# Attention kernel on one core: five of eight value tiles as three fp32r products instead of one fp32 product

## The chip, the cores and the metric

The kernel runs on one core of one Trainium2 chip. The metric is the device time in microseconds of one execution. A core has TensorE (PE: matmuls, and PEld: its weight loads), VectorE (DVE), ScalarE (ACT), GpSimd (POOL) and SyncE (SP, which here only starts DMAs). Each engine works through its own list of instructions in order; semaphores order the engines against each other.

## The reference

One block of a network: gated cross-attention and then a gated feed-forward part with quantised weights. Batch 2, 512 queries of 512 channels, a context of 1024 keys of 128 channels, 16 heads. Cut to what matters (`kv_rope` is both key and value):

```python
q_r = einsum('bshq,hqr->bhsr', q_big, W_qr)        # queries, 64 numbers per head
k_r = einsum('bld,hdr->bhlr', kv_rope, W_kr)       # keys, 64 numbers per head
scores = einsum('bhsr,bhlr->bhsl', q_r, k_r)
attn = softmax(scores)
ctx_c = einsum('bhsl,bld->bhsd', attn, kv_rope)    # the value product
out = einsum('bhsd,hkd->bshk', ctx_c, w_kc_kv).reshape(b, s, H * K) @ Wo.T
x = x + tanh(g_xattn) * out
x = x + tanh(g_ffn) * ffn(layernorm(x))            # rmsnorm, ternary weights, silu gate
```

## The kernel before, in words

**Tiling.** Heads go in eight pairs (p = 0 to 7). A pair has four units (w = 0 to 3): a unit is one batch and half of the queries. A unit's probabilities are four tiles t of 128x1024 in `E`. The main loop walks slots: slot (p, w) has eight steps c = 0 to 7. In it TensorE does the value product of unit w from the turned probabilities `G` (`pv_matmul`, L1383, one key tile of 128 keys for each step, an fp32 product), and everything else works ahead: the second half of unit w + 2 (tiles 2 and 3; "u2") and the first half of unit w + 3 (tiles 0 and 1; "u3").

**One tile's way.** TensorE makes its scores (`score_matmuls`, L1360; two banks `ps_s`, so the scores of the next two tiles wait for the exponentials of the last two). DVE takes the row maximum (`max_tile`, L1755), ACT the exponential with its sum (`exp_tile`, L1580), DVE the reciprocal (`inv_tile`, L1760), GpSimd scales the tile (`pool_scale`, L1160), DVE turns its 32x32 blocks (`turn_blocks`, L1765). When the four tiles of a unit are turned and the value product of the unit that used the buffer is over, SP starts 16 DMAs from `E` to `G` (`exchange`, L1096); the value product of that unit runs in the next slot. The first exponential of u3 waits for that exchange, since it writes `E` again.

**DVE's order in a slot** (`dve_pair`): reciprocal of u3's tile 1 from the slot before, turn tile 0, `ctx_lo`, turn tile 1, low parts of side tasks, maxima of u2's tiles 2 and 3, their reciprocals, turn tile 2, read of an `out` product, turn tile 3, maxima of u3's tiles 0 and 1, another `out` read, reciprocal of tile 0. In pairs 4 to 6 two roundings of feed-forward weights (`round_half`, L1781) stand in front of the turn of tile 2.

**ACT's order** (`act_pair`): `ctx_high` at step 0, high parts of side tasks (`side_high`, L1536), exponentials of u2's tiles 2 and 3 at steps 2 and 3, of u3's tiles 0 and 1 at steps 6 and 7, and two halves of the feed-forward weights: absolute sums in pairs 0 to 3 ("sum") at steps 1 and 4, tanh in pairs 4 to 6 ("quant"), both at step 0.

**GpSimd's order** (`pool_pair`): the scalings of u2's tiles 1, 2, 3 and of u3's tile 0, nothing else but in a few slots.

**Side tasks** on TensorE between the steps, for the next pair: `m` and `a` (query matrix), `q`, `k` (keys: three fp32r products of `wk_hi`, `wk_lo` with `kvT_hi`, `kvT_lo`, L1322 to L1324), `b` (output matrix) and `out` (L1265 to L1267: six fp32r products). An exact fp32 value is kept there as a high part (its fp32r rounding) and a low part (the rest), and a product is high x high, low x high and high x low.

Of the kernel before, what the change touches and what calls it, by code (L numbers as in the profile page):

```python
# [181 lines left out]
def build(nc, A):  # L182
    with ExitStack() as ctx:
# [983 lines left out]
        def xn_low(pool, b):  # L1167

            pool.wait_ge(side_done, side_index(0, "first", ("q", b)) + 1)
            for i in (2 * b, 2 * b + 1):  # L1170
                hi, lo, full = xn_half(i)
                pool.wait_ge(xn_high, i + 1)
                nc.gpsimd.tensor_tensor(lo, full, hi.bitcast(F32), ALU.subtract).then_inc(xn_split, 1)

        def join_xn(pool, b):
# [2 lines left out]
            for h in range(2):
                hi, lo, _ = xn_half(2 * b + h)
                whole = xn_rows[:, b, h * DT // 2:(h + 1) * DT // 2, :].rearrange("p c s -> p (c s)")  # L1180
                nc.gpsimd.tensor_tensor(whole, hi.bitcast(F32), lo.bitcast(F32), ALU.add).then_inc(xn_joined, 1)

        def pool_pair(pool, p, last=False):
            for w in range(4):
                second, first = not (last and w >= 2), not (last and w >= 1)
                for at, t in enumerate((1, 2, 3, 0)):
                    if second if t else first:
                        pool_scale(pool, *unit_ahead(p, w, 2 if t else 3), t)
                    if at == 0:
                        if is0(p) and w in XN_LOW_SLOTS:  # L1190
                            xn_low(pool, XN_LOW_SLOTS.index(w))
                        for b in range(BATCH):
                            if isinstance(p, int) and (p, w) == XN_JOIN_SLOTS[b]:
                                join_xn(pool, b)
                    if last and (w, at) == (1, 2):
                        ln2_root(pool, 0)
                if last and w == 1:
                    atanh_end(pool)
# [798 lines left out]
```

## Time and profile before

| | us |
|---|---|
| median of 3 runs (lowest, highest) | 673.21 (672.68, 674.67) |
| the profiled execution | 677.15 |
| its span, first to last instruction | 675.4 |
| busy PE / DVE / ACT / POOL | 653.5 / 543.9 / 356.8 / 259.7 |
| granted TensorE clock, mean | 0.995 |

The page of the profile gives busy time by engine, the span in 40 slices, the chain of work that ended last, and the costliest groups. The timeline gives each instruction's start, duration and, in brackets, how long its engine stood idle before it and what released it. Durations of matmuls include the time in the array, so the distance between starts is the cost of one. A waiting instruction holds up all that its engine has behind it.

### The profile page before, as it was taken

How to read it: one execution, taken by the hardware profiler on the slowest of the kernel's cores; microseconds unless marked ns; L12 is line 12 of the kernel's file. 1: busy time of each engine (PE TensorE's matmuls, PEld its weight loads, DVE VectorE, ACT ScalarE, POOL GpSimd, SP SyncE). 2: the span in 40 equal slices, each digit the busy share in tenths (PEclk: the TensorE clock that was granted, in tenths of full speed). 3: DMA queues.
4: the chain of work that ended last, by engine and by line, in shares of the span. 5: the costliest groups of instructions: out<-in, count | busy, mean ns of one | idle time of the engine just before them, and what ended most of it. 6: DMA issues, size and time to landing. Idle time of an engine off the chain costs nothing.

```text
span 675.4 us, 9297 instructions
## 1 busy us (share of the span) xinstructions
PE 653.5 (97%) x2870; PEld 377.5 (56%) x2870; DVE 543.9 (81%) x882; ACT 356.8 (53%) x571; POOL 259.7 (38%) x232
## 2 busy tenths in 40 slices
PE   9798999999999999999999999999999898999997
PEld 8564555665665555565655555555555454445553
DVE  5787877788868885888698979997999886998873
ACT  3564664455445544554545454545454533498875
POOL 4822265133223222322235443332333352686651
PEclk9999999999999999999999999999999998999999
DMA  8108885788498849884988688869688763000001
GB/s 299 63 1 218 234 226 117 226 237 228 108 241 243 220 105 243 231 215 109 239 245 207 184 225 237 212 168 238 163 214 230 172 149 101 1 0 32 17 33 48
DMA packets 45206, 112.77 MB, mean 167 GB/s; under 512 B 11888, under 2 KB 15088, under 8 KB 45040
## 3 DMA queue, kind: packets, MB, share of 16 engines
q1 hardware_dynamic: 43712, 110.01, 61.5%
q10 hardware_dynamic: 1392, 2.29, 1.0%
q8 instruction: 19, 0.31, 0.2%
q14 instruction: 19, 0.16, 0.1%
q0 software_dynamic: 64, 0.00, 0.0%
HBM read 45.16 MB, written 2.10 MB: 70 GB/s over the span
## 4 chain that ended last, share of the span: by engine, by line
PE 48%; DVE 30%; ACT 7%; SPq 6%; POOL 3%; issue 3%; DMA 2%; PEld 1%; POOLq 0%; DVEq 0%; ACTq 0%; PEldq 0%
DVE E L1765 9%; PE ps_b L1392 9%; PE ps_s L1371 7%; DVE small L1755 7%; PE ps_ctx L1392 7%; ACT E L1580 6%; SPq L1096 5%; PE ps_s L586 5%; DVE wq L1781 2%; PE ps_b L1265 2%; POOL E L1160 2%; DVE x_sb L1745 2%; PE ps_b L1267 2%; PE ps_b L637 2%; PE ps_b L1266 2%
## 5 line engine op out<-in xcount | busy, mean ns | idle before, releaser
L1160 POOL TENSOR_SCALAR E<-E,small 128x1024 f32<-128x1024 f32 x128 | 151.1, 1190 | 346.7 <-DVE small L1760 346.6
L1580 ACT ACTIVATE E<-ps_s,small 128x1024 f32<-128x1024 f32 x128 | 142.3, 1113 | 209.0 <-DVE small L1755 177.5
L1765 DVE STREAM_TRANSPOSE E<-E 128x1024 f32<-128x1024 f32 x124 | 152.8, 1233 | 27.9 <-POOL E L1160 27.8
L1755 DVE TENSOR_REDUCE small<-ps_s 128x1 f32<-128x1024 f32 x128 | 149.1, 1203 | 4.5 <-PE ps_s L1371 4.4
L1392 PE MATMUL ps_ctx<-G,kv 128*128 128x512 f32 x256 | 123.2, 599 | 0.0
L1392 PE MATMUL ps_b<-G,kv 128*128 128x512 f32 x256 | 119.9, 598 | 2.1 <-DMA G<-E 2.1
L1392 PEld LDWEIGHTS ps_b<-G,kv 128*128 128x128 f32 x256 | 48.0, 190 | 51.8 <-issue 46.0
L1392 PEld LDWEIGHTS ps_ctx<-G,kv 128*128 128x128 f32 x256 | 46.4, 189 | 43.0 <-issue 40.3
L1265 PE MATMUL ps_b<-b_hi,ctx_hi 128*128 128x512 f32 x128 | 66.4, 519 | 0.6 <-DVE ctx_lo L1717 0.6
L1371 PE MATMUL ps_s<-k_hi,q_hi 64*128 64x512 f32 x256 | 57.3, 443 | 4.6 <-ACT E L1580 3.6
L586 PE MATMUL ps_s<-wq,q12T 128*128 128x512 fp8e4 x256 | 61.1, 385 | 0.1
L1371 PE MATMUL ps_s<-k_hi,q_lo 64*128 64x512 f32 x256 | 51.1, 393 | 0.0
L1371 PE MATMUL ps_s<-k_lo,q_hi 64*128 64x512 f32 x256 | 50.8, 392 | 0.0
L1267 PE MATMUL ps_b<-b_lo,ctx_hi 128*128 128x512 f32 x128 | 50.4, 393 | 0.0
L1266 PE MATMUL ps_b<-b_hi,ctx_lo 128*128 128x512 f32 x128 | 50.2, 392 | 0.0
L524 POOL TENSOR_TENSOR hg<-h_f,E 128x512 f32<-128x512 f32 x32 | 40.4, 1270 | 25.1 <-DVE h_f L932 25.1
L1745 DVE SCALAR_TENSOR_TENSOR x_sb<-ps_b,small,x_sb 128x512 f32<-128x512 f32 x62 | 44.6, 720 | 4.7 <-PE ps_b L1267 4.7
L1760 DVE RECIPROCAL small<-small 128x1 f32<-128x1 f32 x128 | 19.3, 156 | 31.0 <-ACT E L1580 24.7
L1371 PEld LDWEIGHTS ps_s<-k_hi,q_hi 64*128 64x128 f32 x256 | 24.1, 183 | 32.6 <-issue 19.1
L586 PEld LDWEIGHTS ps_s<-wq,q12T 128*128 128x128 bf16 x256 | 24.4, 99 | 28.3 <-issue 4.1
L1265 PEld LDWEIGHTS ps_b<-b_hi,ctx_hi 128*128 128x128 f32 x128 | 24.0, 188 | 23.1 <-issue 15.3
L1266 PEld LDWEIGHTS ps_b<-b_hi,ctx_lo 128*128 128x128 f32 x128 | 24.1, 189 | 10.5 <-issue 7.7
(199 smaller groups left out, 960.9 us busy)
## 6 DMA issues: line engine op xcount, KB each, us to landing
G<-E SPq DMA_DIRECT2D x496, 128.0 KB, 2.4
w_stage<-in_wffn SPq DMA_DIRECT2D x48, 512.0 KB, 4.4
wo_s<-in_woT SPq DMA_DIRECT2D x8, 512.0 KB, 5.3
wq_s<-in_wq SPq DMA_DIRECT2D x7, 512.0 KB, 6.3
wkcq_s<-in_wkcqT SPq DMA_DIRECT2D x7, 384.0 KB, 4.5
out<-x_sb SPq DMA_DIRECT2D x8, 256.0 KB, 2.0
x_sb<-in_x SPq DMA_DIRECT2D x3, 512.0 KB, 5.9
wqr_s<-in_wqr SPq DMA_DIRECT2D x7, 192.0 KB, 5.4
```

What stands on the lines that cost most here:

```text
L524: nc.gpsimd.tensor_tensor(hg[:, k, cols], h_f[:, k, cols], g3[:, cols], ALU.mult).then_inc(hg_done, 1)
L586: last = nc.tensor.matmul(ps_s4[:, 2 * i + c % 2, :], q12T[:, k, i, d, :], wq8[:, DT * i + d, cols], start=(d == 0), stop=(d == DT - 1))
L1160: nc.gpsimd.tensor_scalar(e, e, rowinv[:, k:k + 1], 1.0, ALU.mult, ALU.mult).then_inc(scaled, 1)
L1265: nc.tensor.matmul(into, ctx_hi[:, cols], b_hi[:, h, :], start=(h == 0), stop=False)
L1266: nc.tensor.matmul(into, ctx_lo[:, cols], b_hi[:, h, :], start=False, stop=False)
L1267: last = nc.tensor.matmul(into, ctx_hi[:, cols], b_lo[:, h, :], start=False, stop=(h == 1))
L1371: last = nc.tensor.matmul(ps_s[:, h, cols], q[head, b, rows], k[head, b, cols], start=(i == 0), stop=(i == 2))
L1392: last = nc.tensor.matmul(CTX_PS[w % 2].rearrange("p (t i q) -> p t i q", t=ST, i=4), kv[:, w // 2, c, :], turned, start=(c == 0), stop=(c ...
L1580: nc.scalar.activation(out, scores, ACT.Exp, bias=negmax[:, k:k + 1], accum_out=rowsum[:, k:k + 1]).then_inc(exp_done, 1)
L1745: last = nc.vector.scalar_tensor_tensor(x, bank_in, g_tanh[:, 0:1], x, ALU.mult, ALU.add)
L1755: nc.vector.tensor_reduce(negmax[:, k:k + 1], ps_s[:, t % 2, :], AX_X, ALU.max, negate=True).then_inc(max_done, 1)
L1765: nc.vector.transpose(e_tile(w % 2, t), e_tile(w % 2, t)).then_inc(blocks_turned, 1)
```

## The change

It does these things:

- In pairs 0 to 6 the value product of key tiles 0 to 4 is three fp32r products (`kv_hi` x high, `kv_lo` x high, `kv_hi` x low) instead of one fp32 product; tiles 5, 6, 7 stay fp32. The steps take the tiles in the order 5, 0, 6, 1, 2, 3, 7, 4. Pair 7 stays all fp32.
- ACT makes the high part of each of the five tiles (`split_high`, a copy of 128x512), into one of three places; those of tiles 0, 1, 2 at step 0, of tile 3 at step 2 behind the exponential of u2's tile 2, of tile 4 at step 4.
- GpSimd makes the low parts (`split_low`, a subtraction of 128x512). Its order in a slot becomes: scale u2's tile 1, low 0, low 1, low 2, low 3, scale u2's tiles 2 and 3, low 4, scale u3's tile 0. The splitting and joining of `xn` is spread out ahead of the last one.
- GpSimd cuts `kv` in high and low parts before the loop (`cut_kv`) and joins them before pair 7 (`join_kv`).
- The `k` task becomes one fp32 product of the whole `wkr_s` and `kvT`. The high and low parts of the key weights (`wk_high`, `wk_low`) and the low part of `kvT` go away; SP's load of the next key weights waits for the last `k` task, in the third slot.

The diff, cut:

```diff
+SPLIT = 5
+HIGH_PLACE = (0, 2, 1, 0, 1)
+STEP_TILE = (5, 0, 6, 1, 2, 3, 7, 4)
+HIGH_STEPS = (0, 0, 0, 2, 4)
...
+        def split_low(pool, p, w, i):
+            tile = g_tile(w % 2, i)
+            pool.wait_ge(split_hi, SPLIT * 4 * p + (SPLIT * w + i + 1))
+            pool.sem_inc(pool_passed, 1)
+            nc.gpsimd.tensor_tensor(g_tile(w % 2, i, G_lo), tile, high_part(i).bitcast(F32).rearrange("p (t i q) -> p t i q", t=ST, i=4),
+                                    ALU.subtract).then_inc(split_lo, 1)
...
         def pool_pair(pool, p, last=False):
             for w in range(4):
                 second, first = not (last and w >= 2), not (last and w >= 1)
...
+                u2, u3 = unit_ahead(p, w, 2), unit_ahead(p, w, 3)
+                if is0(p) and w == 0:
+                    split_low(pool, p, w, 0)
+                if second:
+                    pool_scale(pool, *u2, 1)
...
+                if not (last or is0(p) and w == 0):
+                    split_low(pool, p, w, 0)
+                if not last:
+                    split_low(pool, p, w, 1)
...
+                if not last:
+                    split_low(pool, p, w, 2)
+                if not last:
+                    split_low(pool, p, w, 3)
+                if second:
+                    pool_scale(pool, *u2, 2)
+                    pool_scale(pool, *u2, 3)
...
+                if not last:
+                    split_low(pool, p, w, 4)
+                for i in range(2 * BATCH):
+                    if is0(p) and w == XN_LOW_SLOTS[i]:
+                        xn_low(pool, i)
+                    if isinstance(p, int) and (p, w) == XN_JOIN_SLOTS[i]:
+                        join_xn(pool, i)
+                if isinstance(p, int) and (p, w) == (PAIRS - 2, 3):
+                    join_kv(pool, 0)
+                if first:
+                    pool_scale(pool, *u3, 0)
...
+            if tile < SPLIT and not (isinstance(p, int) and p == PAIRS - 1):
+                high = high_part(tile).rearrange("p (t i q) -> p t i q", t=ST, i=4)
+                pe.wait_ge(split_lo, SPLIT * 4 * p + (SPLIT * w + tile + 1))
+                nc.tensor.matmul(into, kv_hi[:, b, tile, :], high, start=(c == 0), stop=False)
+                nc.tensor.matmul(into, kv_lo[:, b, tile, :], high, start=False, stop=False)
+                last = nc.tensor.matmul(into, kv_hi[:, b, tile, :], g_tile(w % 2, tile, G_lo), start=False, stop=(c == LT - 1))
+                if tile < SPLIT - 1:
+                    last.then_inc(split_done, 1)
+            else:
+                last = nc.tensor.matmul(into, kv[:, b, tile, :], turned, start=(c == 0), stop=(c == LT - 1))
...
+        def split_high(act, p, w, i):
+            used = 4 * (SPLIT - 1) * p + (SPLIT - 1) * w
+            if i == 0:
+                if is0(p) and w == 0:
+                    act.wait_ge(kv_cut, 6)
+                else:
+                    act.wait_ge(split_done, used)
+                act.wait_ge(exchanged[w % 2], 2 * EXCHANGE * p + EXCHANGE * (w // 2 + 1))
+            elif i == 2:
+                if not (is0(p) and w == 0):
+                    act.wait_ge(pv_done, 4 * p + w)
+            elif i == 3:
+                act.wait_ge(split_done, used + 1)
+            elif i == 4:
+                act.wait_ge(split_done, used + 3)
+            copy_act(high_part(i).rearrange("p (t i q) -> p t i q", t=ST, i=4), g_tile(w % 2, i)).then_inc(split_hi, 1)
...
                 for c in range(LT):
+                    if c == 0 and variant != "last":
+                        split_high(act, p, w, 0)
...
-                    if (w, c) == WK_AT and variant != "last":
-                        wk_high(act, 16 * p + 32)
+                    for i in range(1, SPLIT):
+                        if c == HIGH_STEPS[i] and variant != "last":
+                            split_high(act, p, w, i)
...
-                nc.tensor.matmul(into, wh, kvT_hi[:, b, cols], start=True, stop=False)
-                nc.tensor.matmul(into, wl, kvT_hi[:, b, cols], start=False, stop=False)
-                last = nc.tensor.matmul(into, wh, kvT_lo[:, b, cols], start=False, stop=True)
+                last = nc.tensor.matmul(into, wkr_s[:, :, :].rearrange("p a r -> p (a r)"), kvT[:, b, cols], start=True, stop=True)
...
-                    if (w, c) == WK_AT and variant != "last":
-                        wk_low(dve, p + 2)
```

## Rows read from the trace of the kernel before

**Rows 1.** The page's first part: busy time by engine over the whole span.

```profile
PE 653.5 (97%) x2870; PEld 377.5 (56%) x2870; DVE 543.9 (81%) x882; ACT 356.8 (53%) x571; POOL 259.7 (38%) x232
```

**Rows 2.** Windows, pair 2's four slots: length, busy PE, PEld, DVE, ACT, POOL; clock, DMA.

```profile
182.74:202.53 19.79, 19.79 (x93) 12.65 (x92) 13.83 (x22) 7.56 (x14) 4.46 (x5) 1.00 0.78 206
202.53:218.30 15.77, 15.77 (x66) 9.64 (x65) 13.39 (x19) 8.55 (x16) 4.45 (x5) 1.00 0.89 242
218.30:233.71 15.41, 15.41 (x61) 8.73 (x60) 12.89 (x17) 8.39 (x15) 4.46 (x5) 1.00 0.88 227
233.71:248.71 15.00, 15.00 (x61) 8.75 (x61) 12.39 (x16) 7.91 (x15) 4.47 (x5) 1.00 0.59 133
```

**Rows 3.** The same view, pair 6's four slots.

```profile
452.12:472.01 19.89, 19.48 (x84) 11.37 (x83) 15.24 (x22) 10.32 (x18) 4.73 (x5) 1.00 0.83 218
472.01:488.45 16.44, 16.44 (x65) 9.22 (x63) 15.23 (x20) 7.46 (x13) 5.12 (x5) 1.00 0.60 161
488.45:504.63 16.18, 16.18 (x62) 8.82 (x61) 14.57 (x19) 8.33 (x14) 5.22 (x5) 1.00 0.84 214
504.63:520.22 15.59, 15.59 (x62) 8.31 (x62) 13.97 (x19) 7.81 (x13) 5.22 (x5) 1.00 0.86 232
```

**Rows 4.** The same view, pairs 0, 1, 3, 4 and 5 whole.

```profile
49.46:117.03 67.57, 64.97 (x253) 35.41 (x252) 52.82 (x73) 38.41 (x68) 28.30 (x22) 1.00 0.77 199
117.03:182.74 65.71, 65.71 (x276) 39.51 (x275) 52.59 (x73) 32.13 (x58) 17.85 (x17) 1.00 0.77 204
248.71:316.55 67.84, 66.74 (x281) 40.12 (x280) 53.10 (x76) 32.36 (x59) 17.82 (x16) 1.00 0.77 197
316.55:384.76 68.21, 67.62 (x290) 41.00 (x290) 57.27 (x80) 31.89 (x52) 24.75 (x19) 1.00 0.80 212
384.76:452.12 67.36, 67.20 (x264) 37.34 (x263) 58.64 (x79) 33.78 (x55) 25.53 (x19) 1.00 0.81 215
```

**Rows 5.** Timeline of DVE, the last slot of pair 2.

```profile
237.35 2.35 DVE L1755 TENSOR_REDUCE small<-ps_s 128x1 f32<-128x1024 f32 x2
239.84 0.16 DVE L1760 RECIPROCAL small<-small 128x1 f32<-128x1 f32 x1
241.36 1.25 DVE L1765 STREAM_TRANSPOSE E<-E 128x1024 f32<-128x1024 f32 x1 [0.22 <-POOL E L1160]
248.71 1.25 DVE L1765 STREAM_TRANSPOSE E<-E 128x1024 f32<-128x1024 f32 x1 [0.60 <-POOL E L1160]
```

**Rows 6.** Timeline of ACT and of POOL, the same slot.

```profile
238.61 1.11 ACT L1580 ACTIVATE E<-ps_s,small 128x1024 f32<-128x1024 f32 x1 [1.21 <-DVE small L1755]
...
240.21 2.27 POOL L1160 TENSOR_SCALAR E<-E,small 128x1024 f32<-128x1024 f32 x2 [5.43 <-DVE small L1760]
```

**Rows 7.** Chain of waits: start, length, what; fp32 value products and one fp32r product.

```profile
206.94 3.43 PE ps_b L1392 x8
...
269.29 0.23 PE ps_b L1345
```

**Rows 8.** Groups of instructions: busy us, mean ns; idle before.

```profile
L524 POOL TENSOR_TENSOR hg<-h_f,E 128x512 f32<-128x512 f32 x32 | 40.4, 1270 | 25.1 <-DVE h_f L932 25.1
L1536 ACT ACTIVATE xnT<-xn_rows 128x1024 fp32r<-128x1024 f32 x2 | 2.1, 1052 | 0.0
```

**Rows 9.** Timeline of DVE and ACT, the first slot of pair 2.

```profile
190.25 0.69 DVE L1717 TENSOR_TENSOR a_lo<-ps_b,a_hi 128x512 fp32r<-128x512 f32 x1 [1.84 <-ACT a_hi L1536]
...
197.58 1.11 ACT L1580 ACTIVATE E<-ps_s,small 128x1024 f32<-128x1024 f32 x1 [5.81 <-DMA G<-E]
```

**Rows 10.** Timeline of ACT and DVE, third slot of pair 6: the second `k` task.

```profile
490.69 0.58 ACT L1536 ACTIVATE k_hi<-ps_b 128x512 fp32r<-128x512 f32 x1
...
491.94 0.65 DVE L1717 TENSOR_TENSOR k_lo<-ps_b,k_hi 128x512 fp32r<-128x512 f32 x1
```

**Rows 11.** Instructions of the rounding's line: shortest, median, longest ns; first and last start.

```profile
L1781 DVE TENSOR_SCALAR wq<-w_stage x24: 669/702/1499, 343.5 to 527.5; 128x1024 fp8e4<-128x1024 f32 x24
```

**Rows 12.** Timeline of SP: the 16 DMAs of one exchange.

```profile
217.55 10.04 SPq L1096 DMA_DIRECT2D G<-E  x16
```

More of the change, by code:

```diff
@@ L1124, in sp_pair @@
                     load_wq(sp, p + 2)
-                    sp.wait_ge(wk_ready, p + 2)
+                if w == 2 and not (variant == "last" or isinstance(p, int) and p == 6):
+                    sp.wait_ge(side_done, side_index(p, variant, ("k", 1, 1)) + 1)
                     load_kr(sp, p + 2)
@@ L1165, in xn_half, with xn_low @@
             return tuple(x.rearrange("p c s -> p (c s)") for x in (XNT[b][:, 0, part, :], XNT[b][:, 1, part, :], XNT_FULL[b][:, part, :]))
[L1167 to L1175, printed above, removed]
-            pool.wait_ge(side_done, side_index(XN_JOIN_PAIR, "mid", ("q", b)) + 1)
[L1178 to L1181, printed above, removed]
+        def xn_low(pool, i):
+            pool.wait_ge(side_done, side_index(0, "first", ("q", i // 2)) + 1)
+            hi, lo, full = xn_half(i)
+            pool.wait_ge(xn_high, i + 1)
+            nc.gpsimd.tensor_tensor(lo, full, hi.bitcast(F32), ALU.subtract).then_inc(xn_split, 1)
@@ L1185, in pool_pair @@
                 second, first = not (last and w >= 2), not (last and w >= 1)
[L1186 to L1198, printed above, removed]
+                u2, u3 = unit_ahead(p, w, 2), unit_ahead(p, w, 3)
[3 more added lines that the diff above has]
+                    pool_scale(pool, *u2, 1)
+                if last and w == 0:
+                    join_kv(pool, 1)
+                if not (last or is0(p) and w == 0):
+                    split_low(pool, p, w, 0)
+                if not last:
+                    split_low(pool, p, w, 1)
+                if last and w >= 2:
+                    ln2_root(pool, w - 2)
+                if last and w == 3:
+                    rms_root(pool, 1)
+                if not last:
[5 more added lines that the diff above has]
+                    pool_scale(pool, *u2, 3)
                 if last and w == 2:
@@ L1248, in _ @@
                 pool_scale(pool, 0, 0, t)
-            for t in range(ST):
-                pool_scale(pool, 0, 1, t)
+            cut_kv(pool, 0)
+            pool_scale(pool, 0, 1, 0)
+            pool_scale(pool, 0, 1, 1)
+            cut_kv(pool, 1)
+            pool_scale(pool, 0, 1, 2)
+            pool_scale(pool, 0, 1, 3)
             pool_scale(pool, 0, 2, 0)
@@ L1315, in side_matmuls @@
                 _, b, j = task
[L1316 removed]
+                pe.wait_ge(ld_kr, 16 if at is not None else 16 * p + 32)
                 if at is not None:
@@ L1390, in pv_matmul @@
                     pe.wait_ge(ctx_done, 4 * p + (w - 1))
-            turned = G[:, w % 2, :, :, key_tile(c)].rearrange("p i t q -> p t i q")
-            last = nc.tensor.matmul(CTX_PS[w % 2].rearrange("p (t i q) -> p t i q", t=ST, i=4), kv[:, w // 2, c, :], turned,
-                                    start=(c == 0), stop=(c == LT - 1))
+            b, tile = w // 2, STEP_TILE[c]
+            turned, into = g_tile(w % 2, tile), CTX_PS[w % 2].rearrange("p (t i q) -> p t i q", t=ST, i=4)
+            if isinstance(p, int) and p == PAIRS - 1 and w in (0, 2) and c == 0:
+                pe.wait_ge(kv_joined, b + 1)
+            if tile < SPLIT and not (isinstance(p, int) and p == PAIRS - 1):
[8 more added lines that the diff above has]
+                last = nc.tensor.matmul(into, kv[:, b, tile, :], turned, start=(c == 0), stop=(c == LT - 1))
             if c == LT - 1:
```

86 lines of the change are left out of this document (47 added, 39 removed).

## The prediction

> **What bounds the kernel now.** First the busy times: PE is busy 97% of the span, DVE 81%, GpSimd 38% [rows 1]. Read alone, they say that every matmul saved is time saved. So the next view is the windows, with their edges where DVE turns tile 0 of a slot [rows 2 to 4]. PE is full in pairs 1 and 2 (65.71 us of 65.71 in pair 1) [rows 2, 4]. But DVE, busy only 13.4, 12.9 and 12.4 us in slots of 15.77, 15.41 and 15.00 [rows 2], has to be read by what its gaps wait for, and there the timeline decides. In the last slot of pair 2 DVE takes the two maxima at 237.35, ACT's exponential of tile 2 starts at 238.61, the reciprocal follows at 239.84, GpSimd's scaling at 240.21, DVE's turn of that tile at 241.36, idle until GpSimd was through [rows 5, 6]. That is a loop through DVE, ACT, GpSimd and back, and DVE starts nothing behind that turn before it. The gaps in slots 1 to 3 are all of this kind (a reciprocal that waits for an exponential, a turn that waits for a scaling); none waits for a matmul. Only in slot 0 does DVE wait for outsiders: 1.84 us at the `a` task, and ACT's exponential waits there for the exchange until 197.58, while its maximum was there by 196.6 [rows 9]. So there are two clocks of nearly the same length: PE's work, 66.0 us a pair, and DVE's loop. For the loop of a "sum" pair without outside waits I take slots 1 to 3 as they are (46.2 us) and about 18.6 for slot 0: 64.8. In pairs 4 to 6 the roundings fill DVE's gaps and the loop is the longer clock (68.1 in pair 6, with PE busy 67.7) [rows 3]. Whoever shortens PE alone gains about 1 us a pair; whoever lengthens the loop pays in every slot.
>
> **PE's part.** An fp32 tile costs 3.43 / 4 = 0.858 us (eight records, two a tile), an fp32r product 0.23 us [rows 7]; three make 0.69. Saved: 0.166 us a tile, 20 tiles a pair, 3.3 us; the four `k` tasks go the other way, 0.66 us. Net 2.66 us a pair, 18.6 us over seven pairs. On the path this is worth only what the loop leaves.
>
> **The loop's part.** In a slot GpSimd now does low 0 to 3 between the scaling of tile 1 and that of tile 2. Low 0 to 2 have 5.4 us of idle time to lie in [rows 6]: three subtractions at 1.27 us [rows 8] are 3.8, so they cost nothing. Low 3 doesn't: its high part stands on ACT behind the exponential of tile 2. So the scaling of tile 2, till now 240.21 - 238.61 = 1.60 us behind the start of that exponential [rows 6], comes after: exponential 1.14, high copy 0.6 (the row for twice the size is 1.05; I take 0.6, bounds 0.5 and 0.7), a semaphore's 0.1, low part 1.27 [rows 8]. That is 3.1 us, 1.5 later. The turn of tile 2 moves by the same 1.5, and the read of `out`, the turn of tile 3, the next maxima and exponentials are queued behind it on DVE: all of it shifts. In slot 1 a low part of a `k` task already stands in front of the reciprocal, so only 1.15 is added. In slot 0 two of these low parts (`a`, `k`) hide most of it: I count turn 2 at 9.85 us after turn 0 and 9.2 us from there to the next turn 0, 19.05, about what it was with its waits (19.79) [rows 2]. **Sum pair:** 19.05 + 15.77 + 15.41 + 15.00 + 1.15 + 1.5 + 1.5 = 69.4 us. PE needs 63.3 of these, so it waits now. Pair 1: +3.7, pair 2: +3.4, pair 3 (67.84, it had a late exchange that the idle PE would now absorb): +1.6 [rows 2, 4].
>
> **Quant pairs.** The same, plus two things. ACT has both tanh at step 0 and then the high part of the `k` or `q` task; three high copies now stand in front (1.55 us), and the distance between that task's high part (ready at 491.3) and its low part on DVE (491.94) covers 0.65 [rows 10]: 0.9 us more in slots 2 and 3. And the rounding. It takes 0.67 us with GpSimd silent and up to 1.50 beside it [rows 11]; low 3 now runs where it starts. On the other side the rounding used to fill part of the wait. I take +1.2 for the delay and the roundings, so +2.05 in slot 2 and +2.15 in slot 3, +1.3 in slot 1, +0.3 in slot 0: 5.8 us a pair for pairs 5 and 6. Pair 4 has no tanh in slot 0 and lost time there to an exchange: +4.7. Bounds for each of the nine quant slots: 0.7 (the rounding fills the whole wait) to 2.8.
>
> **Pair 0.** Slots 1 to 3 pay 1.15 + 1.5 + 1.5, and about 0.5 more, because ACT also splits `xn` there. In slot 0 low 0 stands before the scaling of tile 1, and TensorE's scores stand behind the product of tile 0: some 2.7 us, of which the exchange that the next exponential waits for hides a half. Together +6.1; bounds 3 and 9.
>
> **What costs nothing, and its cover.** `cut_kv` on GpSimd, some 3 us twice, lies in idle gaps of about 4 us between scalings. The prologue loses a few low parts on DVE and gets dearer `k` products: 0, within 1.5 either way. `join_kv` (1.6 us) lies in GpSimd's idle time. The `xn` splits before u3's scaling (2.4 us each) fit behind low 4. The later load of the key weights has a slot and more. The exchange needs 10.04 us of SP's starts and some 2.4 to land [rows 12]; slots become longer, so it has more room, and TensorE, now ahead of DVE, frees `G` earlier. Low 4 is ready about 12 us after turn 0, and tile 4 is the last step: TensorE ends a slot some 3 us before DVE, which is enough. Pair 7 and the feed-forward part have no splits: 0.
>
> **The sum.** 6.1 + 3.7 + 3.4 + 1.6 + 4.7 + 5.8 + 5.8 = 31.1 us. The profiled execution, 675.4 of span and 677.15 in all, would become 706.5 and 708.3. It lies 3.9 above the median of the runs; on that, 673.2 + 31.1 = **704.3 us**.
>
> **Rivals.** (1) Faster: the delay of the scaling is not paid, because low 3 gets its high part early or the shift is taken up by idle time that I read as part of the loop. Then the loop stays and only its outside waits go: 1 us a pair in pairs 1 and 2, 3 in pair 3, 1.5 in pair 4, near 666.5; were PE the only clock, 673.2 - 18.6 = 654.6. For it speaks PE at 97%; against it that no gap of slots 1 to 3 names a matmul. It decides below 0.4 us of delay a slot: three slots then use up the 1.2 that slot 0 has. Chance 0.12. (2) The same mechanism at half the price: quant slots at their lower bound of 0.7 (9 slots by 1.1 less, 10 us) and some of pair 0 hidden: 682 to 694. Chance 0.13. (3) Roundings and GpSimd exclude each other. The longest rounding, 1.50 us against 0.67 [rows 11], waited about 0.83 of a scaling that lasts 1.12, which looks like waiting for its end. Then the second rounding of a slot waits for the rest of low 3, or the scaling waits for the rounding, 0.6 more in nine or ten slots: 710. Chance 0.10. The Trainium skill states this as a rule (SBUF — State Buffer, "Who interferes with whom"): a DVE instruction in a 2-port mode and GpSimd take turns whole, the later one fully blocked. By that rule the row is no accident, and the price is this rival's. (4) TensorE falls behind because low 3 or low 4 is late, and the exchange with it: 716 to 728. Chance 0.04. (5) No change: 0.03. That the three products save PE nothing would change none of this, since PE's 66.0 would still be under 69.4.
>
> **How the numbers follow.** Forecast 0.58, at 696 to 712 by the bounds of the copy (0.1 us in 27 slots, 3 us), of the quant slots and of pair 0. The range takes in rival 3 and most of rival 2: 684 to 718, which leaves out 0.12 + 0.04 + 0.03 and a little. Slower by over 0.3% (what a measurement of this kernel can tell from no change): 0.58 + 0.13 + 0.10 + 0.04 = 0.85. Same 0.03, faster 0.12.
>
> **What the new profile would show.** Right: DVE's turn of tile 2 waits for POOL L1160, about 9.3 to 9.9 us after turn 0 where it was 7.65 in the last slot of pair 2; GpSimd's scaling starts right at the end of a low part, 3.1 us behind the start of the exponential; slots 1 to 3 of a sum pair are 16.5 to 17 us long; PE has waits on low parts or exponentials and is below 93% busy; the pair is 69 to 70 in "sum" and 72 to 74 in "quant". Wrong: if the pairs are 63 to 65 us long and PE still full, rival 1; if DVE waits for an exchange or a matmul in slots 1 to 3, rival 4; a low part of 128x512 well under 1.27 us would shrink all terms.

## The result

The changed kernel took **712.5 us** (median of 4 runs, 707.0 to 713.7), beside 673.1 (672.7 to 674.7) for the kernel before: a ratio of 1.0565, 95% interval 1.0508 to 1.0622, so 5 to 6% slower. Its profiled execution took 713.66 us with a span of 711.8.

The profile after, in the order of the views shown of before. The page's first part, busy time by engine (against [rows 1]):

```profile
PE 648.7 (91%) x2978; PEld 399.5 (56%) x2978; DVE 538.4 (76%) x870; ACT 424.5 (60%) x703; POOL 441.6 (62%) x380
```

Windows with their edges at DVE's turn of tile 0 (length, busy PE, PEld, DVE, ACT, POOL, granted clock, DMA share, GB/s): the four slots of pair 2, then of pair 6 (against [rows 2, 3]), then the first slots of pairs 0, 1 and 4:

```profile
197.79:216.80 19.01, 17.31 (x80) 11.40 (x79) 13.64 (x21) 10.65 (x21) 10.68 (x10) 1.00 0.80 217
216.80:233.79 16.99, 16.99 (x74) 10.71 (x74) 13.39 (x19) 10.09 (x19) 10.73 (x10) 1.00 0.87 236
233.79:250.77 16.98, 15.05 (x69) 10.12 (x67) 12.89 (x18) 10.82 (x21) 10.67 (x10) 1.00 0.83 213
250.77:267.15 16.38, 15.17 (x77) 10.23 (x77) 12.29 (x16) 10.19 (x20) 10.70 (x10) 1.00 0.44 100
...
484.43:503.72 19.29, 17.55 (x78) 11.00 (x75) 14.52 (x22) 12.67 (x23) 11.49 (x10) 1.00 0.81 217
503.72:521.46 17.74, 17.74 (x71) 10.29 (x71) 14.82 (x20) 9.97 (x17) 11.25 (x10) 1.00 0.67 173
521.46:539.73 18.27, 15.44 (x65) 9.28 (x61) 14.43 (x19) 10.77 (x19) 11.16 (x10) 1.00 0.72 181
539.73:557.53 17.80, 14.35 (x67) 8.81 (x67) 13.83 (x19) 10.30 (x18) 12.69 (x11) 1.00 0.82 214
...
48.69:73.04 24.35, 19.66 (x77) 11.43 (x76) 13.86 (x21) 13.47 (x26) 11.89 (x11) 0.86 0.73 186
...
124.30:147.44 23.14, 21.46 (x98) 14.82 (x98) 13.95 (x20) 9.95 (x19) 10.73 (x10) 0.93 0.73 197
...
336.89:357.50 20.61, 20.61 (x98) 14.47 (x97) 13.82 (x23) 10.36 (x20) 10.81 (x10) 0.95 0.77 202
```

DVE and TensorE are both less busy and the time is longer: neither is full, both wait. Slots 1 to 3 of pair 2 are 1.2, 1.6 and 1.4 us longer, those of pair 6 1.3, 2.1 and 2.2, and their first slots are 0.8 and 0.6 shorter. The first slots of pairs 0, 1 and 4 are long, and there the granted clock is below 1.00.

What a slot waits for stands in the timeline of its tile 2, here the third slot of pair 2 (ACT, then GpSimd, then DVE; in brackets the idle time and what ended it):

```profile
239.09 1.11 ACT L1674 ACTIVATE E<-ps_s,small 128x1024 f32<-128x1024 f32 x1 [2.05 <-DVE small L1847]
240.20 0.62 ACT L1615 ACTIVATE g_hi<-G 128x512 fp32r<-128x512 f32 x1
```

```profile
241.00 1.26 POOL L1226 TENSOR_TENSOR G_lo<-G,g_hi 128x512 fp32r<-128x512 f32 x1 [2.43 <-ACT g_hi L1615]
242.23 2.24 POOL L1182 TENSOR_SCALAR E<-E,small 128x1024 f32<-128x1024 f32 x2
```

```profile
243.40 1.25 DVE L1857 STREAM_TRANSPOSE E<-E 128x1024 f32<-128x1024 f32 x1 [1.29 <-POOL E L1182]
```

Exponential at 239.09, high copy, low part at 241.00, scaling at 242.23: 3.14 us behind the start of the exponential, where it was 1.60 [rows 6]. GpSimd sits idle for 2.43 us in front of the low part; the wait is for the copy on ACT, which stands behind the exponential. The groups over the whole span (busy us, mean ns; idle before):

```profile
L1226 POOL TENSOR_TENSOR G_lo<-G,g_hi 128x512 fp32r<-128x512 f32 x140 | 178.0, 1289 | 68.5 <-ACT g_hi L1615 66.1
L1857 DVE STREAM_TRANSPOSE E<-E 128x1024 f32<-128x1024 f32 x124 | 153.2, 1236 | 50.8 <-POOL E L1182 50.6
L1615 ACT ACTIVATE g_hi<-G 128x512 fp32r<-128x512 f32 x140 | 84.7, 629 | 0.6
L1438 PE MATMUL ps_s<-k_hi,q_hi 64*128 64x512 f32 x256 | 57.8, 446 | 21.7 <-ACT E L1674 20.6
```

DVE's turns wait 50.6 us for scalings, and TensorE's scores 20.6 us for exponentials, where it was 27.8 and 3.6 in the kernel before: TensorE waits for the loop, not the loop for TensorE.

### The profile page after: what moved, and what is told of

Same layout as the page of the kernel before. It is cut to its first block, busy times and chain, and to the rows that moved or that the text cites. A ratio compares the mean times of both kernels' runs of the same rounds, so it can differ in the third digit from the quotient of the medians.

```text
span 711.8 us, 10097 instructions
## 1 busy us (share of the span) xinstructions
PE 648.7 (91%) x2978; PEld 399.5 (56%) x2978; DVE 538.4 (76%) x870; ACT 424.5 (60%) x703; POOL 441.6 (62%) x380
## 4 chain that ended last, share of the span: by engine, by line
DVE 34%; PE 19%; ACT 16%; issue 13%; POOL 11%; SPq 4%; DMA 1%; DVEq 0%; POOLq 0%; ACTq 0%; PEld 0%
DVE small L1847 11%; DVE E L1857 10%; ACT E L1674 8%; POOL E L1182 7%; PE ps_s L607 5%; SPq L1117 4%; DVE x_sb L1841 3%; ACT g_hi L1615 2%; POOL G_lo L1226 2%; PE ps_b L658 2%; PE ps_s L1438 2%; ACT w_stage L1698 2%; PE ps_b L1408 2%; DVE ctx_lo L1813 1%; DVE k_lo L1813 1%
## 5 line engine op out<-in xcount | busy, mean ns | idle before, releaser
L1182 POOL TENSOR_SCALAR E<-E,small 128x1024 f32<-128x1024 f32 x128 | 149.1, 1177 | 133.9 <-DVE small L1852 133.9
L1226 POOL TENSOR_TENSOR G_lo<-G,g_hi 128x512 fp32r<-128x512 f32 x140 | 178.0, 1289 | 68.5 <-ACT g_hi L1615 66.1
L1857 DVE STREAM_TRANSPOSE E<-E 128x1024 f32<-128x1024 f32 x124 | 153.2, 1236 | 50.8 <-POOL E L1182 50.6
L1615 ACT ACTIVATE g_hi<-G 128x512 fp32r<-128x512 f32 x140 | 84.7, 629 | 0.6
L1438 PE MATMUL ps_s<-k_hi,q_hi 64*128 64x512 f32 x256 | 57.8, 446 | 21.7 <-ACT E L1674 20.6
L1472 PE MATMUL ps_ctx<-G,kv 128*128 128x512 f32 x116 | 60.4, 615 | 3.4 <-POOL xnT L1194 3.1
L1472 PE MATMUL ps_b<-G,kv 128*128 128x512 f32 x116 | 58.7, 594 | 2.0 <-DMA G<-E 2.0
L1336 PE MATMUL ps_b<-b_hi,ctx_hi 128*128 128x512 f32 x128 | 56.7, 443 | 1.1 <-DVE ctx_lo L1813 0.5
L1466 PE MATMUL ps_ctx<-g_hi,kv_hi 128*128 128x512 f32 x70 | 41.8, 598 | 15.8 <-POOL G_lo L1226 15.8
L1338 PE MATMUL ps_b<-b_lo,ctx_hi 128*128 128x512 f32 x128 | 50.6, 395 | 0.0
L1466 PE MATMUL ps_b<-g_hi,kv_hi 128*128 128x512 f32 x70 | 42.9, 613 | 2.6 <-POOL G_lo L1226 2.6
```

The source lines that it names most:

```text
L1182: nc.gpsimd.tensor_scalar(e, e, rowinv[:, k:k + 1], 1.0, ALU.mult, ALU.mult).then_inc(scaled, 1)
L1226: nc.gpsimd.tensor_tensor(g_tile(w % 2, i, G_lo), tile, high_part(i).bitcast(F32).rearrange("p (t i q) -> p t i q", t=ST, i=4), ALU.subtra ...
L1336: nc.tensor.matmul(into, ctx_hi[:, cols], b_hi[:, h, :], start=(h == 0), stop=False)
L1438: last = nc.tensor.matmul(ps_s[:, h, cols], q[head, b, rows], k[head, b, cols], start=(i == 0), stop=(i == 2))
L1466: nc.tensor.matmul(into, kv_hi[:, b, tile, :], high, start=(c == 0), stop=False)
L1472: last = nc.tensor.matmul(into, kv[:, b, tile, :], turned, start=(c == 0), stop=(c == LT - 1))
```

## The experiments

Ten kernels ran. The kernel before was timed again beside them: 673.6 us beside delay_alone, light_products, low3_last and wait_at_q, 674.4 beside whole_products, scores_first, copies_behind and all_four, and 674.5 beside low3_between and five_edits. Ratios are against it. Slots of a pair are numbered 0 to 3, so the third slot is slot 2. Slot lengths below are read as above, between DVE's turns of tile 0.

**The delay alone, in the kernel before (delay_alone).** GpSimd does one operation more, ahead of the scaling of tile 2; TensorE's work is as it was.

```
 for at, t in enumerate((1, 2, 3, 0)):
+    if t == 2 and not last:
+        q, v = unit_ahead(p, w, 2)
+        pool.wait_ge(exp_done, 16 * q + (4 * v + 3))
+        full = kvT_hi[:, 0, 0:EXTRA].bitcast(F32)
+        nc.gpsimd.tensor_tensor(pad[:, :], full, full, ALU.subtract)
```

> The kernel before, whole, with one addition: in pairs 0 to 6 GpSimd waits for the exponential of tile 2 and then does one subtraction of 128x752 (about 1.9 us by the 1.27 us of a 128x512 one) ahead of its scaling of tile 2. No split, no high copy, TensorE unchanged. Theory (DVE's loop): the scaling starts about 3.1 us behind the start of the exponential where it was 1.6, the turn of tile 2 waits for GpSimd, slots 1 to 3 of a sum pair become 16.5 to 17 us long (15.0 to 15.8 before) and the pair 69 to 70; 27 slots pay 0.9 to 1.5 each, so the time is 673.2 + 24 = 697, range 692 to 703, with TensorE idle in every slot although its work is the same. Rival (idle time takes the delay up, TensorE at 97% is the only clock): 673 to 679, slots unchanged.

Measured: 691.1 us, ratio 1.0257 (1.0217 to 1.0296), 17.5 us more. The operation was shorter than I had meant. GpSimd, last slot of pair 2, where the exponential started at 241.77:

```profile
243.06 1.44 POOL L1193 TENSOR_TENSOR pad<-kvT_hi 128x752 bf16<-128x752 f32 x1 [4.94 <-ACT E L1587]
244.48 1.13 POOL L1162 TENSOR_SCALAR E<-E,small 128x1024 f32<-128x1024 f32 x1
```

The scaling lies 2.71 us behind the exponential, 1.11 later than before. Windows of the same pair:

```profile
185.26:204.01 18.75, 17.87 (x75) 10.31 (x74) 13.83 (x21) 7.18 (x13) 5.88 (x6) 1.00 0.80 216
204.01:220.53 16.52, 16.52 (x69) 10.02 (x67) 13.39 (x19) 8.70 (x16) 5.87 (x6) 1.00 0.90 245
220.53:237.06 16.53, 16.41 (x67) 9.74 (x66) 12.89 (x18) 8.02 (x15) 5.86 (x6) 1.00 0.87 216
237.06:252.99 15.93, 15.86 (x73) 9.53 (x73) 12.29 (x16) 8.00 (x15) 5.86 (x6) 1.00 0.47 107
```

Slots 2 and 3 are 1.1 us longer (16.53 and 15.93, against 15.41 and 14.82 in the next experiment, where TensorE's work is lighter), slot 1 is 0.7 longer, the first slot not at all. In slots 2 and 3 the delay of the scaling is paid one to one. The time is below the expected 692 to 703 for two reasons: the delay was 1.1 us and not 1.5, and I had 27 slots pay, where the first slot of a pair pays nothing and slot 1 only in part. The rival (673 to 679) is out.

**TensorE's part alone, in the kernel before (light_products).** The products of tiles 0 to 4 are three fp32r products of operands that lie ready, so the context is another one and there are no splits.

```
-last = nc.tensor.matmul(CTX_PS[w % 2]..., kv[:, w // 2, c, :], turned, start=(c == 0), stop=(c == LT - 1))
+if c < 5 and not (isinstance(p, int) and p == PAIRS - 1):
+    for i in range(3):
+        last = nc.tensor.matmul(CTX_PS[w % 2], kvT_lo[:, w // 2, 0:P], kvT_hi[:, w // 2, 0:NF],
+                                start=(c == 0 and i == 0), stop=False)
```

> The kernel before with TensorE's part of the change alone: in pairs 0 to 6 the products of value tiles 0 to 4 are three fp32r products each, of operands that lie ready in SBUF (the parts of the turned keys), so that there is neither a high copy nor a low part; the context computed is another one. The key tasks stay as they were, so TensorE saves 3.3 us a pair, 23.2 in all. Theory (two clocks of nearly equal length): only what the loop leaves is gained, about 1 us in pairs 1 and 2, 3 in pair 3, 1 to 2 in each other: 664 to 668, with TensorE idle before the scores, waiting for exponentials. Rival (TensorE is the only clock): 673.2 - 23.2 = 650. Rival (three products are no shorter than one fp32): 673, and the three records are not 0.23 us apart.

Measured: 671.1 us, ratio 0.9956 (0.9940 to 0.9973): 2.5 us gained, where TensorE's busy time fell by 22.1 (653.5 to 631.4 over the span; 23.2 expected). Pair 2, first slot to last:

```profile
181.51:200.26 18.75, 18.05 (x88) 12.32 (x88) 13.84 (x22) 7.18 (x13) 4.45 (x5) 1.00 0.79 217
200.26:216.04 15.78, 15.78 (x74) 10.98 (x73) 13.39 (x19) 8.71 (x16) 4.45 (x5) 1.00 0.91 247
216.04:231.45 15.41, 14.23 (x66) 9.69 (x65) 12.89 (x17) 8.00 (x15) 4.46 (x5) 1.00 0.86 225
231.45:246.27 14.82, 14.82 (x74) 10.38 (x73) 12.30 (x17) 7.99 (x15) 4.48 (x5) 1.00 0.58 131
```

They make 64.76 us, my reading of DVE's loop without outside waits. Slots 1 and 2 did not get shorter at all against [rows 2]; pairs 5 and 6 took 67.38 and 68.11, as before. So TensorE as the only clock (650) is out, and so is a product that saves nothing (TensorE's busy time in pair 2 fell by 3.1 us, and the pair by 1.2). I had expected 664 to 668, because pairs 3 and 4 of [rows 4] promised 3 and 1.5 us. In the profiles they are there (pair 3 fell by 2.7 us, pair 4 by 1.3, the span by 6.1), but the profiled execution of before lay 3.9 us above its median. So the late exchanges that they rest on were probably those of that one execution; that is an inference, since no second trace of the kernel before was kept.

**The fourth low part behind the scalings, in the changed kernel (low3_last).**

```
-if not last:
-    split_low(pool, p, w, 3)
 if second:
     pool_scale(pool, *u2, 2)
     pool_scale(pool, *u2, 3)
+if not last:
+    split_low(pool, p, w, 3)
```

> The changed kernel with the fourth low part behind the scalings of tiles 2 and 3 instead of ahead of them; nothing else is moved. Theory (the delay of the scaling is the price): the scaling of tile 2 goes back to about 1.6 us behind the start of the exponential, slots 1 to 3 of sum pairs to 15.2 to 15.8 us and the sum pairs to 65 to 66; 3 pairs by 4, pair 0 by 4, nine quant slots by 1.3 each give back 28: 712.5 - 28 = 684, range 679 to 690. The waits at the start of pairs 0, 1 and 4 stay. Rival (TensorE, which now gets the fourth low part 2 us later, becomes the late one): it waits for the low part of tile 3 at step 5 by 1 us or more a slot and the time stays above 700. Rival (the copies on ACT are the price, not the place of the low part): 705 to 712.

Measured: 686.9 us, ratio 1.0167 (1.0125 to 1.0209): moving this one operation in GpSimd's order gives back 25.6 of the 39 us. Pair 2 is back at 65.34. In the profiles 1.6 of the 25.6 lie in pair 4's first slot, where the clock fell in the changed kernel and did not fall here, and that part is not GpSimd's order. In pair 6 the third slot is still long:

```profile
242.42:257.40 14.98, 14.98 (x75) 10.45 (x74) 12.19 (x16) 10.32 (x20) 10.71 (x10) 1.00 0.57 129
...
497.69:514.79 17.10, 15.32 (x60) 9.46 (x59) 14.29 (x20) 10.77 (x19) 11.38 (x10) 0.90 0.70 177
```

14.98 in the last slot of pair 2 (15.00 before). That TensorE gets the low part 2 us later costs nothing: the first rival is out, and the second with it.

**The fourth low part between the scalings, in the changed kernel (low3_between).** It stands behind the scaling of tile 2 and ahead of that of tile 3.

> The changed kernel with the fourth low part between the scalings of tiles 2 and 3. Theory (each us by which a turn moves is a us of the slot): the turn of tile 2 is back at 7.5 to 8.5 us behind turn 0, and that of tile 3, which stands 1.8 us behind it, waits for a scaling that now ends 2.4 us behind the start of the other turn's scaling end, 0.6 to 0.7 us too late; sum slots 1 to 3 at 16.4, 16.0 and 15.5, and with 27 slots at about 0.9 less than in the changed kernel the time is 712.5 - 24 + 3 = 690, range 687 to 696, between low3_last (686.9) and the changed kernel. Rival (any low part of tile 3 ahead of a scaling costs its whole 1.27 us): 708 to 712.

Measured: 699.1 us, ratio 1.0341 (1.0299 to 1.0384). In sum slots 1 to 3 the mechanism was right to a tenth: 16.36, 16.00 and 15.40 us in pair 2. DVE's turn of tile 3 waits there for 0.34 us:

```profile
238.84 1.25 DVE L1858 STREAM_TRANSPOSE E<-E 128x1024 f32<-128x1024 f32 x1 [0.34 <-POOL E L1182]
```

The total missed its range, through my sum: I took the gain per slot as 0.9, and did not see that the first slot loses something, because the turn of tile 3 moves there too (19.56 after 19.01, 19.87 after 19.29). The quant slots also gained less than the 0.9, 0.6 to 0.7. Pair 2 gained 2.0 us, pair 6 only 1.3.

**TensorE whole again, in the changed kernel (whole_products).** All copies, low parts and waits stay; each split tile is one fp32 product (the high part of the turned keys is left out of the context).

```
-nc.tensor.matmul(into, kv_hi[:, b, tile, :], high, start=(c == 0), stop=False)
-nc.tensor.matmul(into, kv_lo[:, b, tile, :], high, start=False, stop=False)
-last = nc.tensor.matmul(into, kv_hi[:, b, tile, :], g_tile(w % 2, tile, G_lo), start=False, stop=(c == LT - 1))
+last = nc.tensor.matmul(into, kv_hi[:, b, tile, :].bitcast(F32), g_tile(w % 2, tile, G_lo).bitcast(F32), start=(c == 0), stop=(c == LT - 1))
```

> The changed kernel with its high copies, low parts and all its waits, but TensorE multiplies each of the five value tiles by one whole fp32 product of the low parts (0.86 us for three of 0.23), so its 3.3 us a pair are given back: 23.2 us more work over seven pairs. The high part of the turned keys is left out of the context. Theory (the loop sets 69.4 us a pair and TensorE needs 66.6): 712.5 plus or minus 2, slots of pair 2 at 19.0, 17.0, 17.0 and 16.4 as before the edit. Rival (TensorE is the clock of the changed kernel too): 725 to 735.

Measured: 712.3 us (709.1 to 713.9), against 712.5. The page, over the whole span:

```profile
PE 663.7 (93%) x2838; PEld 374.8 (53%) x2838; DVE 538.9 (76%) x870; ACT 425.5 (60%) x703; POOL 440.1 (62%) x380
```

TensorE is busy for 15 us more (I had expected 23), and neither the time nor pair 2 (69.40 us after 69.36) moves. What the change saves on TensorE in the value products is worth nothing in the changed kernel.

**The wait for `xn` where it is needed, in the changed kernel (wait_at_q).** Pair 1's first slot was 4.1 us longer than pair 2's. TensorE waited ahead of all of pair 1 for the low parts of `xn`, two of which stand at the end of pair 0 on GpSimd.

```
-pe.wait_ge(xn_split, 2 * BATCH)
 with pe.Fori(1, 4) as p:
...
 else:
+    pe.wait_ge(xn_split, 2 * BATCH)
     for c in range(DT):
         nc.tensor.matmul(into, a_hi[:, c, :], XNT[b][:, 0, c, :], start=(c == 0), stop=False)
```

> The changed kernel with one wait moved: TensorE waits for the four low parts of xn not at the start of pair 1 but at its first use of them, the q task of slot 1. Theory: the first slot of pair 1 (23.1 us, against 19.0 in pair 2) is long because TensorE stands 3.1 us there, then runs at the granted clock 0.50, and the m task, for which SP holds the exchange, comes late; with the wait moved the clock stays at 1.00, SP starts the exchange within 1 us of turn 0 and the slot is 19 to 19.5 us: 712.5 - 4 = 708.5. Rival (the two splits of xn on GpSimd delay the scaling, and that is the price): the slot stays at 22 to 23 us and the time at 712.

What stands in the changed kernel there: TensorE, then its clock in windows of 2 us, then SP and ACT.

```profile
123.51 1.62 PE L1472 MATMUL ps_ctx<-G,kv 128*128 128x512 f32 x2 [3.14 <-POOL xnT L1194]
```

```profile
121.00:123.00 2.00, 0.00 (x0) 0.00 (x0) 1.37 (x4) 2.00 (x5) 2.00 (x1) 1.00 0.00 0
123.00:125.00 2.00, 1.49 (x3) 0.71 (x4) 0.70 (x1) 1.76 (x4) 2.00 (x3) 0.75 0.00 0
125.00:127.00 2.00, 2.00 (x11) 2.00 (x10) 2.00 (x3) 0.00 (x0) 2.00 (x3) 0.50 0.00 0
```

```profile
129.08 10.07 SPq L1117 DMA_DIRECT2D G<-E  x16
```

```profile
142.49 1.11 ACT L1674 ACTIVATE E<-ps_s,small 128x1024 f32<-128x1024 f32 x1 [6.82 <-DMA G<-E]
```

TensorE idles for 3.1 us, then runs at a granted clock of 0.50 (1.2 of 2.4 GHz) until past 127 us, and so the `m` task, which SP waits for ahead of the exchange, is late; the exchange starts 4.8 us behind turn 0, where in pair 2 it is 0.3 (198.10), and ACT waits 6.8 us for it. With the wait moved the slot is

```profile
123.52:142.52 19.00, 16.49 (x74) 11.02 (x73) 13.64 (x21) 9.83 (x19) 10.65 (x10) 1.00 0.75 202
```

and the time 708.7 us (1.0501, 1.0459 to 1.0542), 3.8 less. GpSimd's splits are where they were, so the rival is out.

**The scores first, in the first slot of pair 0 of the changed kernel (scores_first).**

```
-if is0(p) and (w, c) == (0, SECOND_HALF_STEP):
-    task_first = False
-    pv_matmul(pe, p, w, c)
```

> The changed kernel with one thing moved, in the first slot of pair 0: TensorE does the scores of step 1 ahead of the product of tile 0, which waits for the first low part, and not behind it. Theory (that slot is 24.3 us where 20.0 were, because TensorE stands 3.2 us for the low part and then does the scores at the granted clock 0.50): the scores start at 51 us and not 54.9, the clock is above 0.9 and the slot is 20.5 to 22 us: 712.5 - 3 = 709.5. Rival (the exchange that lands at 64 to 65 us sets the end of the slot anyway, or GpSimd's first low part ahead of its scaling does): 24 us and 712.

In the changed kernel TensorE waits for the first low part, and the scores stand behind its product:

```profile
53.29 0.80 PE L1466 MATMUL ps_ctx<-g_hi,kv_hi 128*128 128x512 f32 x1 [3.24 <-POOL G_lo L1226]
...
54.87 0.79 PE L1438 MATMUL ps_s<-k_hi,q_hi 64*128 64x512 f32 x2
```

They start 2.8 us later than in the kernel before (52.05), at a clock of 0.50, and last 2.9 us instead of 1.7. With the scores first:

```profile
48.82:68.85 20.03, 16.88 (x77) 10.04 (x76) 13.86 (x22) 13.50 (x26) 11.85 (x11) 1.00 0.84 217
```

20.03 us, as in the kernel before (20.02), at a clock of 1.00, and 707.3 us in all (1.0488, 1.0460 to 1.0516): 5.2 less. The whole surplus of that slot, 4.3 us, was this wait and the clock behind it; the exchange hid none of it. My 3 us were too few. This edit takes both away together, but the trace of wait_at_q bears on the clock's part: the same wait of 3.24 us, half as long a stretch at 0.50 (3.4 us instead of 6.8), and a slot of 23.3 us instead of 24.35. It is a hint and no measurement: low3_between, also with 3.4 us at 0.50, took 24.6.

The profile of scores_first also parts the two at the head of pair 1, which this edit leaves alone. TensorE waits there for 3.15 us, as in the changed kernel, but its clock stays at 1.00 through the slot:

```profile
120.08:141.88 21.80, 19.83 (x98) 13.54 (x97) 13.83 (x20) 9.96 (x19) 10.75 (x10) 1.00 0.77 213
```

The exchange starts 3.1 us behind turn 0 (123.21), and the slot is 21.80 us, against 23.14 with the fall of the clock and 19.00 without the wait. Of the 4.1 us that wait_at_q took out, some 2.8 are the wait itself and 1.3 the clock.

**The copies of tiles 1 and 2 behind the high part of the task (copies_behind)**, on top of low3_last.

```
-HIGH_STEPS = (0, 0, 0, 2, 4)
+HIGH_STEPS = (0, 1, 1, 2, 4)
```

> The kernel of the run low3_last (686.9 us) with the high copies of tiles 1 and 2 behind the high part of the k or q task on ACT, at step 1, and not ahead of the two tanh at step 0. Theory (slots 2 and 3 of the quant pairs are 17.1 and 16.6 us there, against 16.2 and 15.6 in the kernel before, because three copies stand in front of that high part and only 0.65 us of them are covered): these slots fall by 0.9 each, six slots, 5.5 us: 681.4, range 679 to 684; slot 1 unchanged. Rival (the low parts of tiles 1 and 2, ready later, now come in front of the scaling of tile 2): no gain in the quant slots and up to 1 us more in each sum slot, 687 to 695.

Measured: 681.9 us, 1.0116 (1.0094 to 1.0139), 5.0 less than low3_last. The third slot of pair 6:

```profile
493.80:510.06 16.26, 14.97 (x63) 8.87 (x63) 14.16 (x19) 10.75 (x19) 11.41 (x10) 1.00 0.79 199
```

17.10 became 16.26 (16.18 before the change). The lower clock of the one row, 0.90, is not the reason: the same slot of pair 5 took 17.10 us in low3_last at a clock of 1.00, and 16.27 here. What the edit takes out is 0.84 us here, and 0.5 to 1.0 in the other five slots.

**All four edits (all_four), and a fifth (five_edits).** First the four together; then, with them, the fourth low part of `xn` moved into pair 1's first slot.

> The changed kernel with the four edits together: the fourth low part behind the two scalings, TensorE's wait for xn at the q task, the scores first in the first slot, the copies of tiles 1 and 2 behind the high part of the k or q task. Theory (the prices add up): 712.5 - 25.6 - 3.8 - 3 - 5.5 = 674.6, range 671 to 679, sum pairs at 65.3 us, quant pairs at 67.5 to 68: no better than the kernel before (673.6), because both stand on DVE's loop (64.8 and 67.4 us a pair), and the light products alone took 671.1. Rival (a price that I took out of one place comes back in another): 680 or more. Rival (TensorE's saving counts after all, once the loop is as it was): below 669.

Measured: 675.8 us, 1.0029 (1.0014 to 1.0044), in the range. The sum pairs take 65.3 to 65.7 us, the quant pairs 67.4 to 68.3. The four measured prices, 25.6, 3.8, 5.2 and 5.0, would have made 672.9; the gain of pair 4's first slot, some 1.6 us, lies in the profiles of the first three of them alike and is counted three times, which can be the difference.

```
-XN_LOW_SLOTS = (1, 2, 3, 3)
+XN_LOW_SLOTS = (1, 2, 3)
+if isinstance(p, int) and (p, w) == (1, 0):
+    xn_low(pool, 3)
```

> The kernel of the run all_four (675.8 us) with one thing more moved: the fourth low part of xn on GpSimd, which stands with the third one ahead of the scaling that opens pair 1 and makes the last slot of pair 0 17.9 us long (DVE's turn idle for 3.0 us), goes into the first slot of pair 1, where GpSimd is idle. Theory: that slot falls to 15.6 to 15.9 us, the first slot of pair 1 stays at 19.0: 675.8 - 2.1 = 673.7, the time of the kernel before within 0.3%. Rival (the slot is held by the first of the two low parts as well): 17 us, 675. Rival (the q task in slot 1 of pair 1 now waits): pair 1 over 66 us, 676.

Measured: 673.8 us, 0.9986 (0.9961 to 1.0011). The last slot of pair 0 is 15.59 us (17.87 in all_four). Pairs 1 to 6 of five_edits take 65.5, 65.3, 65.7, 67.6, 68.3 and 68.1 us: the loop's times with hardly anything on top. So 39 us are taken back by five changes of order, with every product, copy and low part still there, and what is left is the time of the kernel before. It is not faster than that kernel, nor than the light products (671.1), which mark what TensorE's saving brought here without its costs.

## Why the prediction was right, and where it was off

The direction, the mechanism and most of the size were right. The number has some luck in it: 712.5 lies just above the 696 to 712 of the forecast itself, and inside 684 to 718 because that range also took in rival 3, whose price was not paid. What the sum missed are the first slots of pairs 0, 1 and 4, by 2.9, 4.1 and 1.5 us; the smaller misses, most of them the other way, and the place of the two profiled executions among their runs about cancel.

**The bound.** Right. The loop without outside waits was put at 64.8 us a pair and measured 64.76; in pairs 5 and 6 TensorE's saving changed nothing. TensorE's own term was about right: with light products its busy time in pair 2 fell from 65.97 to 62.89 us, 3.1 for my 3.3.

**The delay.** The steps of the sum against the profile: high copy 0.63 (0.6), low part 1.29 (1.27), scaling 3.14 behind the exponential (3.1). Pair 2 came out at 69.36 (69.4), its slots at 19.01, 16.99, 16.98 and 16.38. The turn of tile 2 lies 9.6 us behind turn 0 in slots 1 and 2 and 9.03 in slot 3, a little under the 9.3 that I gave as the lower end. That the delay carries the price was shown twice, by adding it to the kernel before and by taking it out of the changed one. Of pair 2 that leaves 0.6 us open (65.34 in low3_last, 64.76 with the light products).

**Quant pairs.** Slots 1 to 3 of pair 6 grew by 1.30, 2.09 and 2.21 us (1.3, 2.05, 2.15); pair 5 as a whole grew by 5.8 (5.8), pair 6 5.0, since its first slot got shorter by 0.6 where I had added 0.3. The 0.9 for the copies measured 0.84 in the third slot of pair 6, and 0.5 to 1.0 elsewhere.

**Pair 0 and its first slot.** Off: 8.0 us instead of 6.1. Slots 1 to 3 cost 3.7 together, less than the 4.65. The first slot cost 4.3 where I had counted 1.4: I halved 2.7 us because "the exchange that the next exponential waits for hides a half". It hid nothing, and the delay of the scores was longer than I thought: they start 2.8 us late, the granted clock is 0.50 behind the idle time, and they last 2.9 us instead of 1.7.

**Pair 1.** The largest miss: 7.8 us instead of 3.7. I wrote that the `xn` splits "fit behind low 4", which is true of GpSimd's time in slots 1 and 2, but the last slot of pair 0 has two of them, and I never asked who waits: TensorE, at the head of pair 1, then the `m` task, SP's exchange and the next exponential. The wait stood there in the kernel before too and cost nothing; the change made what it waits for late. By scores_first some 2.8 us of the 4.1 are that chain, and 1.3 the lower clock on top.

**Pair 4.** 6.2 instead of 4.7; the 1.5 us are again a first slot at a clock of 0.95, behind 2.0 us in which TensorE waits. Here the clock is all of it: with the same wait and a clock of 1.00, in wait_at_q and scores_first, pair 4 grew by 4.6. In the kernel before TensorE came to that matmul without a wait; now it is ahead of DVE, whose read of `out` the matmul follows.

**The rest.** Pair 3 1.9 (1.6); the prologue -0.8 and pair 7 with the feed-forward part -0.8, where I had 0 for both. The changes between the two spans make 36.4 us, against 31.1; the medians lie 39.4 apart, because the profiled execution of before lay 3.9 above its median and that of after only 1.2 above its own.

**Rival 3.** The roundings did not get dearer; their mean fell from 920 ns to 771:

```profile
L1873 DVE TENSOR_SCALAR wq<-w_stage 128x1024 fp8e4<-128x1024 f32 x24 | 18.5, 771 | 0.0
```

But its mechanism is in the trace. GpSimd and DVE, second slot of pair 6:

```profile
511.12 1.40 POOL L1226 TENSOR_TENSOR G_lo<-G,g_hi 128x512 fp32r<-128x512 f32 x1 [2.62 <-ACT g_hi L1615]
512.50 2.67 POOL L1182 TENSOR_SCALAR E<-E,small 128x1024 f32<-128x1024 f32 x2
```

```profile
512.23 0.85 DVE L1873 TENSOR_SCALAR wq<-w_stage 128x1024 fp8e4<-128x1024 f32 x1
```

The rounding starts 0.3 us before the low part ends and lasts 0.85 instead of 0.67; the two scalings, which start with 0.58 us of the rounding left, take 2.67 instead of 2.23. It is plainer in delay_alone, whose roundings have a mean of 1414 ns. There a rounding starts with 1.06 us of GpSimd's subtraction left and lasts 0.94 us longer than 0.67 (second slot of pair 6):

```profile
489.37 1.44 POOL L1193 TENSOR_TENSOR pad<-kvT_hi 128x752 bf16<-128x752 f32 x1 [5.56 <-ACT E L1587]
489.75 1.61 DVE L1788 TENSOR_SCALAR wq<-w_stage 128x1024 fp8e4<-128x1024 f32 x1
```

The Trainium skill's rule (SBUF — State Buffer, "Who interferes with whom"), that of a DVE instruction in a 2-port mode and one of GpSimd the later is held until the earlier is done, agrees with these rows in kind; in size the later one pays a good half or more of what is left, 0.18 of 0.29 us, 0.44 of 0.58 and 0.94 of 1.06. That the rival's 0.6 us are not in the time has a likely reason: the kernel before had paid already. In the same slot its second rounding lasts 1.36 us and its two scalings 2.91, more than in the changed kernel. That slot grew by 1.30 us, my 1.3; no run isolates the part of the exclusion in it.

## What to carry to other kernels

When two engines have clocks of nearly the same length, take work off one only after you know what the other's loop waits for; a light version of the saved work, without its costs, tells in one run what the saving can bring (here 2.5 us of 22). Put added work on a helper engine behind whatever the loop is waiting for, even where the helper is idle for most of the time: here GpSimd was busy 38% of the time before and 62% after, and the place of one 1.3 us operation cost some 24 us. And for every wait that a change adds, or whose signal it makes later, follow it to the next engine and the next transfer, above all at a loop's entry.

## What the hardware showed that I had not expected

TensorE's granted clock fell to 0.50 around idle stretches of 3.1 and 3.2 us (pairs 1 and 0) and was back at 1.00 some 4 and 6 us after work went on. It did not do so each time: at the head of pair 1 TensorE was idle for 3.15 us in scores_first and for 3.02 in copies_behind, and the clock stayed at 1.00 through both slots. Nor does it take as long a wait. At one other place, the mean's matmul ahead of pair 4, TensorE waited for 2.0 us both in the changed kernel and in wait_at_q; in the first the clock fell, in the second it stayed (the matmul and the window behind it, for each):

```profile
335.24 0.37 PE L1487 MATMUL ps_b<-small 128*128 128x24 f32 x2 [2.01 <-DVE x_sb L1841]
```

```profile
336.00:338.00 2.00, 2.00 (x6) 1.19 (x5) 1.93 (x5) 1.76 (x4) 1.31 (x2) 0.50 0.03 8
```

```profile
330.29 0.37 PE L1488 MATMUL ps_b<-small 128*128 128x24 f32 x2 [2.02 <-DVE x_sb L1841]
```

```profile
331.00:333.00 2.00, 2.00 (x16) 1.62 (x16) 1.93 (x5) 1.82 (x4) 1.31 (x2) 1.00 0.05 8
```

That slot was 20.6 us in the one and 19.0 in the other. Such falls are likely also behind the spread of the changed kernel's own runs (707.0 at a mean clock of 0.990, 712.0 to 713.7 at 0.982 to 0.985), which I didn't test further. Last, GpSimd's subtraction of 128x752 with a bf16 output took 1.44 us, less than the 1.9 that the 1.27 us of a 128x512 one with an fp32 output would make; whether the output type, a fixed part or its two inputs, which are the same tensor, is the reason stays open.
